# A state-space block with a mixture-of-experts FFN on one core: all eight experts for every token, against only the two that a token is routed to

## Chip, core and metric

The kernel runs on one core of one Trainium2 chip. The metric is the device time of one execution in microseconds (us).

## The reference, cut to what matters

```python
# x: (4, 1024, 512) float32, T = 4096 tokens, D = 512, 8 experts of 256 hidden units, top 2
mod = (_silu(L0_c) @ L0_wmod).reshape(4, 6, 1, -1)       # sa, ca, ga, sb, cb, gb
h = _layernorm(x) * (1 + ca) + sa
x = x + ga * _L0_attn_ref(h, ...)      # conv of 4 taps, projections, softplus, then a scan over
                                       # the 1024 tokens: h = dA * h + dBu, 16 states per channel
h = _layernorm(x) * (1 + cb) + sb
x = x + gb * _L0_ffn_ref(h, ...)

# _L0_ffn_ref
logits = jnp.tanh(xt @ Wg1.T) @ Wg2.T
_, top_idx = jax.lax.top_k(logits, 2)
top_scores = jax.nn.softmax(top_logits, axis=1)
scores = jnp.zeros_like(logits).at[rows, top_idx].set(top_scores)
up = jnp.einsum('td,ehd->teh', xt, Wup) + bup            # every expert for every token
h = jax.nn.silu(up)
down = jnp.einsum('teh,eoh->teo', h, Wdown) + bdown
out = jnp.einsum('te,teo->to', scores, down)             # six of eight scores are zero
```

## The kernel before

The 4096 tokens are cut into 8 chunks of 512 (`NC`), each with two half chunks `cs` of 256 tokens for the FFN (`NF` = 16). The state-space part ("attention" in the code) of a chunk has 64 slots: 16 states times 4 blocks of 128 channels. In a slot ScalarE makes the decay by an exponential into a bank of PSUM (`da`, L1065), GpSimd multiplies `DU` with the broadcast row `BR` into one of four `DB` buffers (`dbu`, L837), VectorE scans both over the 512 tokens (`scan`, L1297), TensorE transposes the result in four pieces (`flip`, L1563), and VectorE multiplies and adds it to `ACC` (`acc`, L1322). The last chunk is split: two scans of 256 in each slot (L1302).

All engines walk one list, `order`, made by `schedule()`: a task stands at a half slot `h`, and 128 half slots (2 W) are one chunk of the scan. Every engine takes its own tasks out of the list in that order and waits on semaphores for the others. So a task that waits holds up whatever stands behind it on its engine; on SyncE this is the queue of all DMAs. Positions are written out by hand in tables: `ATTENTION` for the next chunk's preparation (convolution, projections), `ROUTER` for layer norm, transposes and the gate of a half chunk, `PAIR`/`PAIRS` for its FFN.

The FFN of a half chunk goes expert by expert: for each of 16 blocks `m` of 128 hidden units, `up` (L1612 to L1614) makes the product from weights and tokens split into high and low float32r parts (12 matmuls of 256 columns), ScalarE and VectorE make the SiLU times the token's score (`th` L1167, `t1` L1172, `ys` L1371 with the score row `SR` fetched by a DMA), GpSimd multiplies (`g`, L860), and `dn` (L1642) adds the block into two banks `DN` in float32. For the last blocks `dn` is made of float32r parts instead (`wh`, `wl` L1357, `gh`, `gl` L1363, L1633 to L1635). Then `to` (L1382) applies the gate and `fin` (L865) adds to `ACC`, which a DMA stores. Up weights stay in SBUF; the down weights come again for each half chunk (`WD`, 128 DMAs).

Of the kernel before, what the change touches and what calls it, by code (L numbers as in the profile page):

```python
# [14 lines left out]
LAG = 6
F0 = 24
# [55 lines left out]
    "final": {"fst": (17, 24), "nmf": 26, "fsu": (24, 24), "frs": 26, "fxn": (29, 30), "ftr": (36, 41),
             "fev": (44, 47), "hh": 50, "hl": (49, 61), "r1": 66, "r12": 78, "r2": 82, "r22": 76, "r3": 82,
             "r31": 89, "e1": 91, "r4": 94, "r41": 97, "r42": 97, "sel1": 99, "sel2": 99, "r5": 101, "r52": 101,
             "sw": 103},
    "last": {"fst": (15, 21), "nmf": 26, "fsu": (25, 25), "frs": 31, "fxn": (37, 46), "ftr": (49, 55),
             "fev": (52, 56), "hh": 62, "hl": (58, 64), "r1": 57, "r12": 57, "r2": 58, "r22": 60, "r3": 67,
             "r31": 68, "e1": 67, "r4": 68, "r41": 75, "r42": 75, "sel1": 74, "sel2": 77, "r5": 80, "r52": 79,
             "sw": 80},
    "split": {"fst": (-46, -44), "nmf": -44, "fsu": (-39, -39), "frs": -42, "fxn": (-39, -37), "ftr": (-35, -29),  # L80
             "fev": (-32, -30), "hh": -27, "hl": (-22, -20), "r1": -25, "r12": -24, "r2": -17, "r22": -19, "r3": -19,
             "r31": -19, "e1": -17, "r4": -17, "r41": -16, "r42": -14, "sel1": -12, "sel2": -11, "r5": -9,
             "r52": -12, "sw": -7}}
# [3 lines left out]

PAIR = {"sr": -1, "wd": -4, "up": (0, 2), "th": (4, 4), "ys": (6, 6), "t1": (4, 6), "g": (9, 9), "dn": (12, 14),
        "to": (16, 18), "fin": (18, 22), "out": (17, 25), "gbl": 30, "xa": 25}
FAST = {"sr": -5, "wd": -3, "up": (0, 2), "th": (3, 3), "ys": (4, 4), "t1": (3, 3), "g": (4, 6), "dn": (10, 13),  # L90
        "to": (14, 14), "fin": (19, 27), "out": (35, 35), "gbl": 21, "xa": 21}
TAIL = {"sr": -9, "wd": -11, "up": (-2, -1), "th": (3, 3), "ys": (6, 7), "t1": (4, 5), "g": (7, 7), "dn": (1, 14),
        "to": (16, 19), "fin": (18, 21), "out": (12, 29), "gbl": -4, "xa": 37}
PAIRS = [47, 54, 63, 73, 81, 89, 97, 108, 114, 122, 129, 137, 146, 153, 162, 167]
FAST_PAIRS = [48, 61, 66, 72, 78, 85, 89, 94, 105, 111, 118, 124, 128, 136, 151, 163]
# [1588 lines left out]
```

## Time and profile before

| | |
|---|---|
| time, median of 2 runs | 1391.43 us (1390.89 to 1391.97) |
| span of the profiled execution | 1389.7 us, so the runs shown lie 1.2 to 2.3 us above it |
| busy PE, DVE, POOL, ACT | 94%, 88%, 82%, 71% |
| first scan starts, last scan ends | 43.7 us, 1253.9 us |
| mean granted TensorE clock | 0.977 of 2.4 GHz |

Busy times of PE count matmuls to their modelled ends and overlap each other. The time of a piece on PE is better read from the distance of starts.

### The profile page before, as it was taken

Reading aid. Unit: us, or ns where it says so; the run is one execution under the profiler, and the core shown is the slowest. Engines: PE = TensorE matmul, PEld = TensorE weight load, DVE = VectorE, ACT = ScalarE, POOL = GpSimd, SP = SyncE. Lnnn points to the kernel's source line nnn. Section 1 sums busy time; section 2 is a strip of 40 time slices with the busy share of each in tenths; the row PEclk is TensorE's granted clock in tenths of the full one; section 3 lists DMA queues with packets and bytes.
Section 4 is the critical chain, followed back from the end, with each engine's and each line's share of the span. In section 5 each row is a group of like instructions: output and inputs, shape, how many; then the busy total and the mean of one; then the engine's idle time right before and its main releaser. Section 6 shows DMA issues by size and latency. Waiting matters only on the chain. (4 is left out here: it accounts for less than half of the span.)

```text
span 1389.7 us, 23827 instructions
## 1 busy us (share of the span) xinstructions
PE 1310.4 (94%) x7664; PEld 977.8 (70%) x7664; DVE 1228.5 (88%) x1729; ACT 988.3 (71%) x2110; POOL 1136.4 (82%) x1177
## 2 busy tenths in 40 slices
PE   8888768999999999999999999999999999989998
PEld 4466546767776777777776777767776776768897
DVE  4899999989998999989998999999998999885565
ACT  4875786588857786588858786688758775745654
POOL 1799889799997999799998999799988987762332
PEclk9999867999999999999999999999999999999999
DMA  5542112325342424434342434334253423323342
GB/s 201 177 154 62 61 39 90 115 78 170 94 148 86 161 97 123 132 111 156 90 144 85 164 97 125 125 113 146 87 148 100 129 85 116 108 74 125 112 125 79
DMA packets 99284, 160.94 MB, mean 116 GB/s; under 512 B 9276, under 2 KB 33980, under 8 KB 99160
## 3 DMA queue, kind: packets, MB, share of 16 engines
q1 hardware_dynamic: 99160, 159.42, 36.3%
q8 instruction: 61, 1.00, 0.3%
q14 instruction: 63, 0.52, 0.1%
HBM read 150.60 MB, written 8.79 MB: 115 GB/s over the span
## 5 line engine op out<-in xcount | busy, mean ns | idle before, releaser
L837 POOL TENSOR_TENSOR DB<-DU,BR 128x512 f32<-128x512 f32 x448 | 576.6, 1304 | 43.6 <-DVE H L1297 36.7
L1322 DVE SCALAR_TENSOR_TENSOR ACC<-pb,CTM,ACC 128x512 f32<-128x512 f32 x512 | 373.6, 730 | 42.4 <-PE pb L1563 41.5
L1642 PE MATMUL pb<-WD,G 128*128 128x512 f32 x856 | 406.0, 594 | 0.0
L1065 ACT ACTIVATE pb<-DELP,AN 128x512 f32<-128x512 f32 x448 | 305.8, 685 | 107.5 <-DVE H L1297 105.3
L1563 PE MATMUL pb<-ID,H 128*128 128x128 f32 x2048 | 311.9, 280 | 32.9 <-DVE ACC L1322 25.3
L1563 PEld LDWEIGHTS pb<-ID,H 128*128 128x128 f32 x2048 | 244.0, 144 | 137.0 <-issue 77.5
L1612 PE MATMUL pb<-H2H,WUH 128*128 128x256 f32 x1024 | 326.7, 319 | 12.0 <-DVE TY L1371 11.8
L1297 DVE TENSOR_TENSOR_SCAN H<-pb,DB 128x512 f32<-128x512 f32 x256 | 309.7, 1211 | 13.4 <-ACT pb L1065 12.3
L1614 PE MATMUL pb<-H2H,WUL 128*128 128x256 f32 x1024 | 290.5, 284 | 0.0
L1613 PE MATMUL pb<-H2L,WUH 128*128 128x256 f32 x1024 | 290.2, 283 | 0.0
L860 POOL TENSOR_TENSOR G<-TY 128x256 f32<-128x256 f32 x256 | 188.9, 756 | 99.7 <-ACT TY L1172 44.3
L1297 DVE TENSOR_TENSOR_SCAN H<-pb,ST,DB 128x512 f32<-128x512 f32 x192 | 244.1, 1271 | 7.3 <-ACT pb L1065 7.3
L1642 PEld LDWEIGHTS pb<-WD,G 128*128 128x128 f32 x856 | 149.3, 191 | 108.7 <-issue 107.5
L1612 PEld LDWEIGHTS pb<-H2H,WUH 128*128 128x128 f32 x1024 | 196.3, 192 | 36.2 <-issue 26.4
L1167 ACT ACTIVATE TY<-pb,BUPH 128x256 f32<-128x256 f32 x256 | 108.8, 469 | 149.5 <-PE pb L1614 137.2
L1613 PEld LDWEIGHTS pb<-H2L,WUH 128*128 128x128 f32 x1024 | 196.9, 192 | 13.3 <-issue 12.7
L1614 PEld LDWEIGHTS pb<-H2H,WUL 128*128 128x128 f32 x1024 | 196.2, 192 | 0.0
L1371 DVE SCALAR_TENSOR_TENSOR TY<-pb,BUP,SR 128x256 f32<-128x256 f32 x256 | 110.5, 472 | 35.7 <-ACT TY L1167 32.8
L1172 ACT ACTIVATE TY<-TY 128x256 f32<-128x256 f32 x256 | 102.1, 412 | 0.0
L1302 DVE TENSOR_TENSOR_SCAN H<-pb,ST,DB 128x256 f32<-128x256 f32 x128 | 88.4, 732 | 6.4 <-ACT pb L1070 4.3
L840 POOL TENSOR_TENSOR DB<-DU,BR 128x512 f32<-128x512 f32 x64 | 81.2, 1281 | 4.1 <-DVE H L1302 4.1
L1256 DVE SCALAR_TENSOR_TENSOR U<-DELP,PV,U 128x512 f32<-128x512 f32 x57 | 59.6, 1059 | 0.8
(220 smaller groups left out, 1700.0 us busy)
## 6 DMA issues: line engine op xcount, KB each, us to landing
WD<-in_wdT SPq DMA_DIRECT2D x128, 512.0 KB, 4.7
BR<-bscr SPq DMA_DIRECT2D x112, 256.0 KB, 3.7
SR<-sscr SPq DMA_DIRECT2D x128, 128.0 KB, 4.6
ACC<-in_x SPq DMA_DIRECT2D x16, 512.0 KB, 4.0
out<-ACC SPq DMA_DIRECT2D x32, 256.0 KB, 3.0
DU<-in_x SPq DMA_DIRECT2D x7, 1024.0 KB, 5.6
BR<-bscr SPq DMA_DIRECT2D x32, 128.0 KB, 3.1
DU<-in_xpT SPq DMA_DIRECT2D x7, 320.0 KB, 3.1
```

What stands on the lines that cost most here:

```text
L837: eng.tensor_tensor(DB[:, i % NDB], DU[:, c % 2, r], BR[:, n % 2], ALU.mult).then_inc(S["dbu"], 1)
L860: eng.tensor_tensor(G[:, i % NG], TH[:, m % 2], YS[:, m % 2], ALU.mult).then_inc(S["g"], 1)
L1065: eng.activation(DA[i % NDA][:], DEL[:, c % 2, r], ACT.Exp, scale=AN[:, r, n:n + 1]).then_inc(S["da"], 1)
L1167: eng.activation(TH[:, m % 2], up_of(cs, m), ACT.Tanh, scale=0.5, bias=BUPH[:, m:m + 1]).then_inc(S["th"], 1)
L1297: eng.tensor_tensor_scan(H[:, (c * NS + n) % NH, r], DA[i % NDA][:], DB[:, i % NDB], ST[:, n, r:r + 1] if state_from(c, h) else 0.0, ALU.mult,
L1322: eng.scalar_tensor_tensor(out=acc, in0=banks[bank_of["flip", c, n, r]][:], scalar=1.0 if n < 0 else CTM[:, c % 2, j, st:st + 1], in1=acc, ...
L1371: eng.scalar_tensor_tensor(out=YS[:, m % 2], in0=up_of(cs, m), scalar=BUP[:, m:m + 1], in1=SR[:, m // 2 % 2], op0=ALU.add, op1=ALU.mult).t ...
L1563: t = eng.transpose(b[:, dt * 128:dt * 128 + 128], src[:, dt, r * 128:r * 128 + 128], ID[:])
L1612: eng.matmul(b, WUH[:, kk, sl], H2H[:, cs % 2, kk], start=kk == 0, stop=False)
L1613: eng.matmul(b, WUH[:, kk, sl], H2L[:, cs % 2, kk], start=False, stop=False)
L1614: t = eng.matmul(b, WUL[:, kk, sl], H2H[:, cs % 2, kk], start=False, stop=kk == 3)
L1642: eng.matmul(DN[j][:], G[:, (cs * NM + m) % NG, j * 128:j * 128 + 128], WD[:, (cs * NE + m // 2) % NWD, m % 2], start=False, stop=m == NM ...
```

## The change

The FFN is made only for the chosen pairs of token and expert. The 16 half chunks form 6 groups (4, 4, 4, 2, 1 and 1 half chunks; `GROUPS`). When a group is routed, VectorE and TensorE work out for each of its two choices a row number such that the rows of one expert fill slots of 128 (`s1` to `s8`, `rk`), and GpSimd scatters each block of 128 tokens twice, 2064 bytes a row (the normed token and its score), into a DRAM buffer `xdr` by indirect DMA (`sc`). A group has as many tiles of 128 rows as it can need at worst: 23, 23, 23, 15, 11 and 11, together 106. For each tile: load (`xl`), transpose (`xt`, `xe`), bias and 4 float32 matmuls of 256 columns (`up`, `uq`) against weights that lie in SBUF at an address read from a register (`tile_expert`), tanh and product for two tiles at once (`th`, `gg`), transpose (`gt`, `ge`), bias and 2 float32 matmuls of 512 columns (`dn`, `dq`), scaling by the score (`ye`) and store to `ydr` (`yst`). Then for every block of 128 tokens GpSimd gathers the two results by indirect DMA, the second adding to the first (`yg`), multiplies by the gate (`zm`) and adds to `x` (`fin`); `x` was parked in DRAM for chunks 0 to 5 (`x1s`, `xr`). The high and low splits, the score rows and the DMAs of the down weights are gone.

```diff
+GROUPS = ((0, 1, 2, 3), (4, 5, 6, 7), (8, 9, 10, 11), (12, 13), (14,), (15,))
+SORT = {"e0": 2, "e1": 3, "e2": 5, "e3": 6, "s1": 2, "s2": 4, "rk": 5, "s3": 7, "s4": 8, "s5": 9, "s6": 10, "s7": 11, "s8": 13,
+        "c1": 14, "c2": 14, "c3": 15, "c4": 15, "sc0": 15, "e4": 22, "sc1": 24}
+SORT_AT = (50, 50, 50, 50, -22, 50)
+TILE = {"xl": (0, 2), "xt": (8, 10), "xe": (11, 13), "up": (15, 17), "uq": (16, 18), "th": 21, "gg": 24, "gt": 27, "ge": 30,
+        "dn": (33, 36), "dq": (34, 37), "ye": (37, 40), "yst": (41, 44)}
+PAIRS = ([335, 351, 367, 383, 399, 415, 431, 447, 463, 479, 495, 511],
+         [590, 606, 622, 638, 654, 670, 686, 702, 718, 734, 750, 766],
+         [845, 855, 865, 875, 885, 895, 905, 915, 925, 935, 945, 955],
+         [970, 980, 990, 1000, 1010, 1020, 1030, 1040],
+         [1055, 1065, 1075, 1085, 1095, 1105],
+         [1118, 1128, 1138, 1148, 1158, 1168])
+BACK = {"yg0": 0, "xr": 0, "yg1": 4, "zm": 8, "fin": 9, "out": 11}
+BACKS = ([556, 562, 568, 574, 580, 586, 592, 598],
+         [811, 817, 823, 829, 835, 841, 847, 853],
+         [1000, 1006, 1012, 1018, 1024, 1030, 1036, 1042],
+         [1085, 1091, 1097, 1103],
+         [1150, 1156],
+         [1213, 1219])
...
+    return (256 * len(tokens(g)) + NE * 127) // 128
...
+        if what in ("sc0", "sc1"):
+            at += [(h + t // 2, ("sc", g, int(what[2]), t)) for t in range(len(tokens(g)))]
...
+        def tile_expert(g, i):
+
+            return nc.values_load(EID[0:1, g, i:i + 1], engines=[mybir.EngineType.PE], min_val=0, max_val=(NE - 1) * 1024,
...
+                elif what == "xl":
+                    g, i = k
+                    m = tile_no(g, i)
+                    if i == 0:
+                        eng.wait_ge(S["d_sc"], 16 * scatters(g + 1))
...
+                    eng.indirect_dma_start(out=xdr[g % NXD][0:128 * n_tiles(g), :],
+                                           out_offset=bass.IndirectOffsetOnAxis(ap=POS[:, g, way, t:t + 1], axis=0),
+                                           in_=HT[:, t], in_offset=None).then_inc(S["d_sc"], 16)
...
+                    if way:
+                        eng.wait_ge(S[f"d_g{b % 2}"], 32 * (b // 2) + 16)
...
+                    if way:
+                        eng.indirect_dma_start(out=Z[:, b % 2], out_offset=None, in_=rows, in_offset=at_rows,
+                                               compute_op=ALU.add).then_inc(S[f"d_g{b % 2}"], 16)
...
+                elif what == "zm":
+                    g, t = k
+                    b = back_no(g, t)
+                    eng.wait_ge(S[f"d_g{b % 2}"], 32 * (b // 2 + 1))
...
+                elif what == "e4":
+                    g = k[0]
+                    n = len(tokens(g))
+                    eng.wait_ge(S["d_sc"], 16 * (scatters(g) + n))
...
+                elif what == "up":
+                    g, i = k
+                    m = tile_no(g, i)
...
+                    first = tile_expert(g, i)
+                    if i % 2 == 0:
+                        eng.wait_ge(S["gg"], pair_no(g, i // 2))
+                    eng.wait_ge(S["xe"], m + 1)
+                    b = UPB[:, i % 2 * FT:i % 2 * FT + FT]
+                    eng.matmul(b, OHT[:, g, i:i + 1].to_broadcast([64, 128]), BRW[:, 0:FT], start=True, stop=False)
+                    for kk in range(2):
+                        eng.matmul(b, XTS[:, m % 2, kk], WU[:, bass.ds(first + kk * FT, FT)], start=False, stop=False)
...
+                elif what == "dn":
+                    g, i = k
+                    m, p = tile_no(g, i), pair_no(g, i // 2)
+                    first = tile_expert(g, i)
+                    if m:
+                        eng.wait_ge(S["ye"], m)
+                    eng.wait_ge(S["ge"], p + 1)
+                    b = DN[:]
+                    eng.matmul(b, OHT[:, g, i:i + 1].to_broadcast([64, 128]), BRW[:, FT:FT + D], start=True, stop=False)
+                    eng.matmul(b, GT[:, p % 2, 2 * (i % 2)], WD[:, bass.ds(first, D)], start=False, stop=False)
```

`uq` and `dq` read the register again (4 reads for each tile, 424 in all) and make the rest of the matmuls.

## Rows read from the trace of the kernel before

**Rows 1.** Part 1 of the page: busy time of each engine.

```profile
PE 1310.4 (94%) x7664; PEld 977.8 (70%) x7664; DVE 1228.5 (88%) x1729; ACT 988.3 (71%) x2110; POOL 1136.4 (82%) x1177
```

**Rows 2.** Busy time by stretch: chunks 1, 3 and 7, the tail, chunk 0.

```profile
core 0: us, PE busy (x) PEld busy (x) DVE busy (x) ACT busy (x) POOL busy (x), PEclk, DMA share, GB/s
172.40:317.10 144.70, 123.72 (x683) 91.44 (x684) 137.01 (x178) 108.90 (x216) 128.74 (x130) 0.86 0.28 87
471.50:625.00 153.50, 151.16 (x898) 112.41 (x898) 144.70 (x193) 116.12 (x240) 142.63 (x148) 1.00 0.38 124
1087.00:1253.90 166.90, 158.20 (x899) 114.56 (x898) 152.29 (x271) 103.19 (x267) 130.41 (x140) 0.98 0.35 106
1253.90:1389.70 135.80, 129.88 (x811) 113.70 (x810) 76.58 (x136) 75.84 (x189) 43.14 (x54) 1.00 0.35 112
43.70:172.40 128.70, 104.06 (x641) 79.45 (x640) 120.52 (x133) 92.41 (x166) 117.22 (x102) 0.93 0.37 118
```

**Rows 3.** The same view, the start of chunk 1, before its first FFN matmul.

```profile
172.40:205.00 32.60, 21.80 (x98) 14.36 (x99) 32.60 (x39) 28.69 (x62) 27.11 (x31) 0.65 0.12 34
```

**Rows 4.** Timeline of DVE in chunk 0: start, duration, instruction.

```profile
78.72 1.21 DVE L1297 TENSOR_TENSOR_SCAN H<-pb,DB 128x512 f32<-128x512 f32 x1
79.86 0.73 DVE L1322 SCALAR_TENSOR_TENSOR ACC<-pb,CTM,ACC 128x512 f32<-128x512 f32 x1
80.50 1.21 DVE L1297 TENSOR_TENSOR_SCAN H<-pb,DB 128x512 f32<-128x512 f32 x1
```

**Rows 5.** Group of DVE: busy us, mean ns, idle before.

```profile
L1371 DVE SCALAR_TENSOR_TENSOR TY<-pb,BUP,SR 128x256 f32<-128x256 f32 x256 | 110.5, 472 | 35.7 <-ACT TY L1167 32.8 <-DMA SR<-sscr 2.7
```

**Rows 6.** Groups of POOL.

```profile
L837 POOL TENSOR_TENSOR DB<-DU,BR 128x512 f32<-128x512 f32 x448 | 576.6, 1304 | 43.6 <-DVE H L1297 36.7 <-DVE DU L1279 6.1 <-DMA BR<-bscr 0.6
L860 POOL TENSOR_TENSOR G<-TY 128x256 f32<-128x256 f32 x256 | 188.9, 756 | 99.7 <-ACT TY L1172 44.3 <-DVE TY L1371 42.2 <-PE pb L1642 8.7
L808 POOL TENSOR_TENSOR H2L<-XT,H2H 128x512 fp32r<-128x512 f32 x32 | 40.7, 1290 | 8.3 <-DVE H L1302 5.0 <-ACT H2H L1118 3.3
L562 POOL TENSOR_SCALAR S<-IO,IXF,RS 128x104 f32<-128x104 f32 x28 | 20.6, 746 | 0.0
```

**Rows 7.** Pieces of the chain that ended last: start us, us, what.

```profile
1212.36 0.44 PE pb L1572 x4
...
1215.38 1.72 PE pb L1642 x4
1217.10 1.82 PE pb L1582 x8
```

**Rows 8.** Timeline of PE: float32r matmuls, 256 columns, then 512 columns.

```profile
646.26 0.28 PE L1613 MATMUL pb<-H2L,WUH 128*128 128x256 f32 x1
646.38 0.28 PE L1614 MATMUL pb<-H2H,WUL 128*128 128x256 f32 x1
...
1381.03 0.39 PE L1634 MATMUL pb<-WDL,GHL 128*128 128x512 f32 x1
1381.26 0.40 PE L1635 MATMUL pb<-WDH,GHL 128*128 128x512 f32 x1
```

**Rows 9.** DMA issues: KB each, us to landing; then one issue on SyncE's timeline.

```profile
out<-ACC SPq DMA_DIRECT2D x32, 256.0 KB, 3.0
bscr<-H SPq DMA_DIRECT2D x1, 32.0 KB, 1.6
...
645.58 0.32 SPq L644 DMA_DIRECT2D BR<-bscr  x1
```

**Rows 10.** The last pieces of the chain that ended last.

```profile
1385.62 0.70 DVE XT L1382
1386.35 0.69 DVE ACC L1386
```

**Rows 11.** Who waited for whom: us in total, times, longest.

```profile
ACT TY L1167 <- PE pb L1614: 137.2, 72, 5.6
POOL DB L837 <- DVE H L1297: 36.7, 59, 1.3
```

More of the change, by code:

```diff
@@ L72 @@
[L72 to L95, printed above, removed]
@@ L167, in attention_places, with group_of, tokens, place_of @@
     return at
+def group_of(cs):
+    return next(g for g, of in enumerate(GROUPS) if cs in of)
+def tokens(g):
+    return [(cs, j) for cs in GROUPS[g] for j in range(2)]
+def place_of(cs, j):
+    return tokens(group_of(cs)).index((cs, j))
+def n_tiles(g):
+    return (256 * len(tokens(g)) + NE * 127) // 128
+def n_pairs(g):
+    return (n_tiles(g) + 1) // 2
+def tiles_of(g, q):
+    return range(2 * q, min(2 * q + 2, n_tiles(g)))
+def pair_no(g, q):
+    return sum(n_pairs(x) for x in range(g)) + q
+def tile_no(g, i):
+    return sum(n_tiles(x) for x in range(g)) + i
+def back_no(g, t):
+    return sum(len(tokens(x)) for x in range(g)) + t
+def bounced(cs):
+    return cs // 2 < NC - 2
+def scatters(g):
+    return sum(2 * len(tokens(x)) for x in range(g))
 def router_places(cs):
     at = []
-    kind = "even" if cs % 2 == 0 else "last" if cs // 2 == NC - 2 else "odd"
-    if cs // 2 in SPLIT:
-        kind = "final" if cs % 2 else "split"
+    kind = "odd" if cs % 2 else "split" if cs // 2 in SPLIT else "even"
     for what, places in ROUTER[kind].items():
+        if what == "x1s" and not bounced(cs):
+            continue
         if isinstance(places, tuple):
@@ L180, in router_places, with group_places @@
     return at
+def group_places(g):
+    at = []
+    for what, h in SORT.items():
+        h += SORT_AT[g] + 2 * W * (GROUPS[g][-1] // 2 + 1)
+        if what in ("sc0", "sc1"):
+            at += [(h + t // 2, ("sc", g, int(what[2]), t)) for t in range(len(tokens(g)))]
+        else:
+            at.append((h, (what, g)))
+    at.append((max(PAIRS[g][0] + 16, PAIRS[g - 1][-1] + 42 if g else 0), ("xs", g)))
+    if g in (1, 2, 3):
+        at.append((BACKS[g][0] - 4, ("gbl", g)))
+    for q, b in enumerate(PAIRS[g]):
+        for what, h in TILE.items():
+            if isinstance(h, tuple):
+                at += [(b + h[i % 2], (what, g, i)) for i in tiles_of(g, q)]
+            else:
+                at.append((b + h, (what, g, q)))
+    for t, (cs, _) in enumerate(tokens(g)):
+        for what, h in BACK.items():
+            if what == "xr" and not bounced(cs):
+                continue
+            h += BACKS[g][t]
+            at.append((h, ("yg", g, t, int(what[2])) if what in ("yg0", "yg1") else (what, g, t)))
+    return at
@@ L436, in adaln_kernel @@
                 early = at[EMPTIED[what][0], *k] < at["scan", 1, 0, 0]
-                b = min(range(2, 7) if early else range(2, 5), key=lambda b: last[b])
+                b = min(range(2, 7) if early else WORK_BANKS, key=lambda b: last[b])
                 bank_of[task], freed[task] = b, held[b]
@@ L709, in _ @@
+            for q in range(2):
+                eng.wait_ge(S[f"d_o{q}"], 16 * 2 * NC)
             eng.wait_ge(S["d_bw"], 16 * NC)
-            eng.wait_ge(S["d_sw"], 16 * NF)
         @block.gpsimd
```

886 lines of the change are left out of this document (450 added, 436 removed).

## The prediction

> **What bounds the kernel now.** I read the shares of busy time first [rows 1]: PE, DVE and POOL all stand above 80%, so the page alone names no bound. The view by stretch tells more [rows 2]. I cut it at the first scan of each chunk. The reader is to see three regimes: chunk 0, without FFN, 128.7 us; chunk 1, with half an FFN, 144.7; chunks 2 to 6, of which chunk 3 stands for all, some 154 each; then the split last chunk, 166.9; and after the last scan a tail of 135.8 with nothing but FFN. With the 43.7 us of the head that is the span of 1389.7.
>
> PE's busy time overstates, so I price its work by the distance of starts. A float32 matmul of 512 columns takes 0.86 us (two in 1.72), one of 256 columns 0.455 (four in 1.82), a block of four transposes 0.44 [rows 7]; a float32r matmul takes 0.12 at 256 columns and 0.23 at 512 [rows 8]. Counting the list, chunk 3 has 32 `up` x 12 x 0.12 = 46, 64 `dn` x 0.86 = 55, 68 `flip` x 0.44 = 30, and some 11 for the rest: 142 of 154 us. DVE is busy 144.7 and POOL 142.6 in the same stretch. So three engines share the bound, and ACT waits for PE (137 us in total) while POOL waits for the scan (37) [rows 11]. Taking the FFN from PE alone would give only what DVE and POOL allow.
>
> What DVE allows can be read off. Where it never idles, one slot takes 80.50 - 78.72 = 1.78 us (1.14 scan, 0.64 acc) [rows 4]. At the start of chunk 1, before its FFN, DVE is busy for all of 32.6 us although the granted clock is 0.65, a mixture of 1.2 and 2.4 GHz [rows 3]: an idle PE and its slow clock cost the scan nothing there. 64 slots, 5 accs of the skip term and 7 of the convolution give 64 x 1.78 + 5 x 0.64 + 7 x 0.9 + 5 = 128 us for a chunk without FFN, which chunk 0 confirms (128.7 with 8 us of starting stalls and less preparation).
>
> **The change, part by part.** All sums are against the span of 1389.7.
>
> *PE work.* A tile costs `up`+`uq` 4 x 0.455 + 0.12 = 1.94, `dn`+`dq` 2 x 0.86 + 0.23 = 1.95, transposes 0.44 + 0.22: 4.55 us. 106 tiles are 482 us, against 16 x (256 / 16 x 12 x 0.12 + 32 x 0.86) = 809 before. The saving is 40%, not 75%: the worst-case number of tiles is 106 where 64 full ones would do, and the tiles run in float32.
>
> *Where the tiles lie.* From the list: chunk 1 has none, chunks 2 to 7 have 5, 16, 8, 16, 9 and 23 `up`, and 29 `up` and 33 `dn` come after the last scan. In chunks 2 to 6 PE has at most 16 x 4.55 + 30 + 12 = 115 us, so it is no bound. In chunk 7 it has 23 x 4.55 + 30 + 12 = 147, and the tail is PE's again.
>
> *DVE.* `ys` goes (110.5 / 256 = 0.43 each, 14 of the 144.7 us of a full chunk [rows 5]), and `to` (4 x 0.7 [rows 10]). It gains `gg`, 0.65 for two tiles, and about 20 small ones of 0.15 for each sort, 3 us. So chunk 1 gets its floor, 128 + 2 = 130 (-15). Chunks 3 and 5, with 8 `gg`, get 128 + 5 + 1 for the gate + 5 idle, the half of what it idles today: 139 (-15 each).
>
> *POOL.* `g` goes (32 x 0.74 = 24 a chunk), the low parts (4 x 1.29 = 5) and the selection (8 of about 0.75 and small ones, 8) [rows 6]: 142.6 falls to 106. It gains `zm`, 1.3 each, and 128 indirect DMAs. No row shows one. Call its time on POOL X. The lower bound is SyncE's issue of a plain DMA, 0.32 us; the upper is a whole landing of 256 KB, 3.0 [rows 9]. I take 1.1, between POOL's passes over 256 and 512 columns (0.76 and 1.30 [rows 6]), since an entry must be made for each of 128 rows on both sides. The Trainium skill, DMA: Bandwidth & Descriptors, section SWDGE vs HWDGE vs iDMA, says that GpSimd's processor computes the entries in a program loop, with slower setup than the queues that hardware serves; no run here shows that yet. By that page's fit of 2.0 us + bytes / 436e3 a block of 256 KB would land after 2.6 us, an estimate; the landing of 3.0 in rows 9 is what I use.
>
> These DMAs come in bursts, in time order with the `dbu` that the scan needs, and `dbu` is only two slots ahead. *Scatter of 8 blocks:* eight stand within 4 half slots, then `e4` on DVE, 7 half slots after the first, waits for all eight to land, with the scans queued behind it. POOL needs 8 X + 3.5 x 1.27 for `dbu` + 3.0 to land; DVE would be there after 7. Stall 8 X + 0.4 less about 1 for the start = 8.2. The other eight: 8 X + 4.4 against 7 and two slots of lead (3.6): 2.6. Together some 11. *Gather of 8 blocks:* in the 53 half slots of `BACKS` POOL has 27 `dbu` (34 us), 8 `zm` and 8 `fin` (21), 3 of small ones and 16 X = 18, together 76, where DVE needs 27 x 1.78 + 6 = 54 and the lead is worth 5: stall 17 us. The scatters of the next group stand in the same stretch and add to it.
> Chunk 2: 128 + 1 + 3 + 4 idle + 11 = 147 (-7). Chunks 4 and 6: 128 + 3 + 3 + 4 + 11 + 17 = 166 (+12 each). So POOL eats up in every second chunk what PE and DVE give in the others.
>
> *Chunk 7.* PE 147, and some idle as today (166.9 with a like sum of 141 + 8): DVE loses `wl`, `gl` and `ys`, so PE's sum decides more nearly: 156 (-11).
>
> *Tail.* PE after the last scan: 33 x 1.95 + 29 x 1.94 + 27 x 0.44 + 17 x 0.44 + 7 flips, router and `rk` 6 = 146. Today's tail has 41 x 1.44 for `up` and 88 `dn` of mostly 0.69, some 130 in all, and ends 4.7 us after the last matmul [rows 7, 8, 10]: it measures 135.8, so PE runs there with almost no stall. The new end is longer: `ye` 0.6, store 3.0, two gathers one behind the other 2 x (X + 2.2), two rounds of `zm` and `fin` 5, the other block's gather 3, the last store 3: 21 us. With 7 for the waits of group 5's routing, which PE passes in its fixed order: 174 (+38).
>
> *Hidden at nothing:* loading and zeroing (69 stores of 264 KB in chunks 0 to 2) lie on a DMA share of 0.35 [rows 2]; without that cover they would cost about 1 us each. In `up` and `dn` the reads of the register stand ahead of the waits, so they run while PE works off what is queued. Their price is in no row: the lower bound is 0, the upper the shortest trip to memory and back, 1.6 us [rows 9], for some 4 x 54 = 216 reads in chunk 7 and the tail. I take 0. The Trainium skill, Runtime: NRT & Kernel Launch, section Instruction fetch mechanics, gives about 200 ns for loading one register, which the sequencer waits for; if all of these were exposed, 216 x 0.2 = 43 us would come on top, an estimate, and no row shows it.
> SyncE: `xl` waits for the scatters and `out` for `fin`, with the `BR` rows of the scan queued behind; these are fetched 4 slots early (7 us), which covers it while POOL is late by no more.
>
> **Sum.** -15 - 7 - 15 + 12 - 15 + 12 - 11 + 38 = -1: span 1389, time 1390. That is no change.
>
> **Rivals.**
> 1. *Indirect DMAs are cheap on POOL* (X about 0.32 to 0.6). At 0.32: scatter 3, gather 4, so chunk 2 139, chunks 4 and 6 144 each, chunk 7 153, tail 170: -15 - 15 - 15 - 10 - 15 - 10 - 14 + 34 = -60, 1330; at 0.6 about 1351. For it: SyncE's 0.32 for a DMA of the same size. Against it: the row numbers must be read and worked on.
> 2. *Register reads and addresses from registers stall PE* (slower). If each of the 4 reads for a tile holds PE for 0.5 us, chunk 7 and the tail get 216 x 0.5 = 108 longer, chunks 3 and 5 become PE's with 115 + 32 against 139, 8 each: 1390 + 108 + 16 = 1514; at 0.2, 1433. It decides from about 0.12 us each. For it: PE has no slack in the tail today. Against it: the reads precede the waits.
> 3. *X is large, or POOL's waits chain* (slower). At X = 1.8 scatter costs 23 and gather 28: +4, +34, +34, with chunk 7 -5 and the tail +42, 1455. It decides from X = 1.4. The wait of the second gather for the first, with `dbu` behind it, works in the same sense.
> 4. *The clock falls* in chunks 1 and 2, where PE does little. Rows 3 show it at 0.65 with DVE never idle, so I give it no price.
> That fewer tiles are computed than before is certain from the list, so "it doesn't do what it says" is no case.
>
> **How the numbers follow.** Forecast 0.38, rival 1 0.30, rival 2 0.17, rival 3 0.15. The range takes in rival 1's low end and rival 3 and the lower part of rival 2: 1325 to 1465. The forecast's own range is 1365 to 1415. Two per cent is 28 us: faster by more than that 0.33, within it 0.34, slower 0.33.
>
> **What the profile after would show.** Right: chunks 3 and 5 near 139 and DVE almost without idle; chunks 4 and 6 longer than 154, with DVE's idle put down to POOL's `dbu`; an idle of DVE at `e4` released by a DMA; PE back to back in the tail, and some 20 us from its last matmul to the end. It would be wrong if the indirect DMA takes under 0.6 or over 1.5 us on POOL, if PE has gaps at each `up`/`dn` in the tail, or if the tail is under 160.

## The result, and the profile after

The changed kernel takes 1595.24 us (1594.51 to 1595.98, two runs), against 1391.43 before (1390.89 to 1391.97): a ratio of 1.146, 95% interval 1.144 to 1.149. The forecast was 1390 us, its range 1325 to 1465. The profiled execution's span is 1592.8 us.

Part 1 of the page, busy shares, to be held against [rows 1]:

```profile
PE 1211.0 (76%) x5756; PEld 829.7 (52%) x5756; DVE 1128.7 (71%) x1489; ACT 931.1 (58%) x1772; POOL 1027.0 (64%) x936
```

All engines are busy for less time than before, in a longer span: the loss is waiting. The view by stretch says where, one row for each chunk and the last for the tail, against [rows 2]; columns as there:

```profile
43.30:173.60 130.30, 104.29 (x644) 81.77 (x643) 119.37 (x133) 84.86 (x158) 97.52 (x86) 0.90 0.65 194
173.60:303.30 129.70, 86.29 (x391) 61.95 (x390) 127.27 (x154) 94.22 (x168) 102.46 (x92) 0.68 0.45 147
303.30:461.40 158.10, 102.94 (x491) 75.95 (x492) 133.99 (x174) 100.64 (x194) 119.80 (x111) 0.73 0.32 97
461.40:632.50 171.10, 148.03 (x716) 101.02 (x715) 136.00 (x163) 118.04 (x215) 101.48 (x92) 0.94 0.29 97
632.50:829.60 197.10, 118.37 (x553) 84.53 (x551) 140.75 (x175) 105.94 (x204) 157.52 (x140) 0.74 0.42 121
829.60:990.70 161.10, 141.20 (x714) 96.05 (x713) 137.49 (x162) 117.75 (x215) 102.18 (x93) 0.98 0.32 106
990.70:1191.80 201.10, 122.39 (x585) 86.96 (x585) 145.11 (x177) 107.61 (x208) 158.87 (x141) 0.79 0.44 126
1191.80:1376.80 185.00, 174.65 (x862) 118.95 (x860) 144.70 (x263) 116.37 (x263) 104.24 (x98) 0.98 0.39 116
1376.80:1592.80 216.00, 174.26 (x657) 104.14 (x656) 19.90 (x50) 60.49 (x112) 75.72 (x65) 0.92 0.48 137
```

Measured against forecast: chunk 0 130 (129, as before), chunk 1 130 (130), chunk 2 158 (147), chunk 3 171 (139), chunk 4 197 (166), chunk 5 161 (139), chunk 6 201 (166), chunk 7 185 (156), tail 216 (174). Against before the differences are +2, -15, +4, +18, +43, +7, +47, +18 and +80: with the head, which is as long as before, the 203 us by which the span grew. Two patterns are to be seen. In chunks 4 and 6 POOL is the busiest engine (157.52 and 158.87 us) while PE has 118 and 122. In chunks 3, 5 and 7 PE is the busiest: 148, 141 and 175. The granted clock is lower than before as well: chunk 3 had 1.00 and has 0.94, the tail 1.00 and 0.92.

The waits (who waited for whom, total us, times, longest) name both:

```profile
DVE ACC L1376 <- PE pb L1668: 104.3, 79, 4.7
DVE H L1351 <- POOL DB L914: 78.7, 29, 9.4
...
POOL Z L902 <- DMA Z<-ydr,POS: 36.3, 15, 3.5
...
ACT YO L1221 <- DMA ydr<-YO: 35.2, 6, 9.6
...
DVE HT L1422 <- DMA xdr<-HT,POS: 24.6, 5, 7.9
```

The scan's wait for `DB` is new in kind; before, POOL waited for the scan [rows 11]. POOL's groups price the indirect DMA, which no row of before showed (scatter; gather that adds; gather that doesn't; busy us, mean ns, idle before):

```profile
L872 POOL DMA_INDIRECT xdr<-HT,POS x64 | 63.4, 990 | 38.6 <-issue 28.5 <-DVE POS L1462 3.7 <-DVE H L1356 2.9
L891 POOL DMA_INDIRECT Z<-ydr,POS x32 | 51.6, 1612 | 18.9 <-DMA Z<-ydr,POS 12.9 <-issue 4.0 <-DVE HT L1422 0.2
L894 POOL DMA_INDIRECT Z<-ydr,POS x32 | 33.6, 1050 | 85.5 <-issue 49.1 <-DMA ydr<-YO 30.2 <-ACT DU L1045 6.1
```

The DMA issues, against [rows 9] (median us to landing at the end):

```profile
xdr<-HT,POS POOLq DMA_INDIRECT x64, 3.7
Z<-ydr,POS POOLq DMA_INDIRECT x64, 5.0
```

POOL's timeline in chunk 4 shows how they meet the scan (start, us, instruction, idle before):

```profile
748.13 1.87 POOL L914 TENSOR_TENSOR DB<-DU,BR 128x512 f32<-128x512 f32 x1
750.17 1.00 POOL L894 DMA_INDIRECT Z<-ydr,POS  x1 [0.16 <-issue]
...
755.36 0.97 POOL L872 DMA_INDIRECT xdr<-HT,POS  x1 [0.30 <-issue]
756.36 1.27 POOL L914 TENSOR_TENSOR DB<-DU,BR 128x512 f32<-128x512 f32 x1
```

and DVE's timeline the scan that was kept waiting:

```profile
757.83 1.22 DVE L1351 TENSOR_TENSOR_SCAN H<-pb,DB 128x512 f32<-128x512 f32 x1 [5.92 <-POOL DB L914]
```

Five indirect DMAs, a gather of one group and four scatters of the next, stand between two `dbu`: 6.4 us of POOL, and DVE idles for 5.92.

### The profile page after: what moved, and what is told of

The parts are those of the page before. It is cut to its first block and busy times, and to the rows that moved or that the text cites. A ratio compares the mean times of both kernels' runs of the same rounds, so it can differ in the third digit from the quotient of the medians.

```text
span 1592.8 us, 20071 instructions
## 1 busy us (share of the span) xinstructions
PE 1211.0 (76%) x5756; PEld 829.7 (52%) x5756; DVE 1128.7 (71%) x1489; ACT 931.1 (58%) x1772; POOL 1027.0 (64%) x936
## 5 line engine op out<-in xcount | busy, mean ns | idle before, releaser
L1668 PE MATMUL pb<-ID,H 128*128 128x128 f32 x2048 | 360.2, 313 | 184.6 <-DVE ACC L1376 146.9
L1221 ACT ACTIVATE YO<-pb,SCO 128x512 f32<-128x512 f32 x106 | 72.3, 682 | 164.4 <-PE pb L1771 129.0
L1490 DVE SCALAR_TENSOR_TENSOR TH<-TH,pb 128x512 f32<-128x512 f32 (+1 forms) x56 | 36.2, 646 | 133.1 <-ACT TH L1203 133.1
L1741 PE MATMUL pb<-WU,XTS 128*128 x424 | 127.2, 425 | 0.0
L1766 PE MATMUL pb<-WD,GT 128*128 x212 | 123.5, 665 | 0.0
L1748 PE MATMUL pb<-WU,XTS 128*128 x424 | 114.9, 395 | 0.0
L1771 PE MATMUL pb<-WD,GT 128*128 x212 | 110.2, 602 | 0.0
L1748 PEld LDWEIGHTS pb<-WU,XTS 128*128 128x128 f32 x424 | 83.7, 201 | 35.0 <-issue 26.0
L1724 PE MATMUL pb<-ID,XS 128*128 128x128 f32 x424 | 66.5, 284 | 31.2 <-DMA XS<-xdr 14.8
L894 POOL DMA_INDIRECT Z<-ydr,POS x32 | 33.6, 1050 | 85.5 <-issue 49.1
L872 POOL DMA_INDIRECT xdr<-HT,POS x64 | 63.4, 990 | 38.6 <-issue 28.5
L1741 PEld LDWEIGHTS pb<-WU,XTS 128*128 128x128 f32 x424 | 76.2, 200 | 21.1 <-issue 2.0
L1724 PEld LDWEIGHTS pb<-ID,XS 128*128 128x128 f32 x424 | 51.7, 146 | 46.5 <-issue 25.8
L1765 PE MATMUL pb<-BRW,OHT 64*128 64x512 f32 x106 | 53.2, 501 | 28.2 <-ACT YO L1221 23.0
```

The costliest lines, as they stand in the source:

```text
L1668: t = eng.transpose(b[:, dt * 128:dt * 128 + 128], src[:, dt, r * 128:r * 128 + 128], ID[:])
L1724: t = eng.transpose(b[:, dt * 128:dt * 128 + 128], XS[:, m % NXS, dt * 128:dt * 128 + 128], ID[:])
L1741: eng.matmul(b, XTS[:, m % 2, kk], WU[:, bass.ds(first + kk * FT, FT)], start=False, stop=False)
L1748: t = eng.matmul(b, XTS[:, m % 2, kk], WU[:, bass.ds(first + kk * FT, FT)], start=False, stop=kk == 3)
L1766: eng.matmul(b, GT[:, p % 2, 2 * (i % 2)], WD[:, bass.ds(first, D)], start=False, stop=False)
L1771: eng.matmul(DN[:], GT[:, p % 2, 2 * (i % 2) + 1], WD[:, bass.ds(first + D, D)], start=False, stop=True).then_inc(S["dn"], 1)
```

## The experiments

Each kernel is the changed one with one edit, unless said otherwise. Times compare with 1595.24; all but the last are single runs, and before, on the same chips, gave 1390.03 to 1392.68, so that a few us of the whole time say nothing. In the diffs "..." shortens a line. I quote the time from the first scan of a chunk to that of the next.

**1. Register reads.** The offset of the expert's weights is a constant, not read from memory.

```diff
-            return nc.values_load(EID[0:1, g, i:i + 1], ...)
+            return i % NE * 1024
```

> Leaves out the choice of the expert: each tile takes its weights at a constant address (tile number modulo 8) where the changed kernel reads a register four times a tile; all else stays, so the output is another. Theory A (register reads and register addresses hold PE up in chunk 7 and in the tail, where a pair of tiles takes 10.45 us against 9.1 by the prices of the kernel before): the pair falls to about 9.2 us, tail and chunk 7 together lose some 27 pairs x 1.2 = 32 us, the time some 1560. Rival (the reads run ahead of PE's queue and cost nothing): within 4 us of 1595.

1595.35 us, chunk by chunk within 2 us of the changed kernel. Rival 2 is dead: the reads cost nothing. The Trainium skill, Runtime: NRT & Kernel Launch, section Instruction fetch mechanics, gives about 200 ns for such a load; all exposed, that would be 43 us, an estimate. The runs show none of it: the loads are hidden here, most likely since PE's sequencer runs ahead (argued, not shown).

**2. The bias matmuls.** Both are left out.

```diff
-                    eng.matmul(b, OHT[:, g, i:i + 1].to_broadcast([64, 128]), BRW[:, 0:FT], start=True, stop=False)
-                    eng.matmul(b, OHT[:, g, i:i + 1].to_broadcast([64, 128]), BRW[:, FT:FT + D], start=True, stop=False)
```

> Leaves out the two bias matmuls of each tile (212 float32r matmuls with a stationary operand of 64 rows). In the trace the bias of 512 columns holds PE for 0.43 us and that of 256 columns for 0.30, where I had counted 0.23 and 0.12, and the float32 matmul behind it takes 0.2 more than its twin. Theory B (these switches are what the tile costs above my price): a pair of tiles loses 2 x (0.43 + 0.30 + 0.3) = 2 us, 10.45 to about 8.4, tail and chunk 7 some 50 us less, 1545. Rival (PE is held by waits for other engines in the tail, not by its own work): under 20 us.

1531.41 us: 64 less for two instructions priced at 0.35 us a tile together, which would be 37 for all 106. Chunk 3 falls from 171 to 152, chunk 5 from 161 to 148. That is below theory B's 1545; some of chunk 3's fall is the clock's (0.94 before the edit, 0.97 with it; see edit 6). PE's work stands in the way in these chunks, and the matmuls cost more than their own time.

**3. Bias on 128 rows.** They use 64 of the array's rows, all others 128. This kernel widens them, with zeros in the added rows.

```diff
-        BRW = sb("BRW", [64, FT + D], f32r)
+        BRW = sb("BRW", [128, FT + D], f32r)
-        OHT = sb("OHT", [64, len(GROUPS), 23], f32r)
+        OHT = sb("OHT", [128, len(GROUPS), 23], f32r)
-    ...to_broadcast([64, 128])
+    ...to_broadcast([128, 128])
```

> The same work; the one-hot and the bias rows have 128 rows instead of 64 (rows 64 to 127 are zero), so that the bias matmuls use the whole array like their neighbours. Without them a pair of tiles took 8.08 us instead of 10.45 in the tail, 1.18 a tile where two float32r matmuls of 256 and 512 columns should take 0.35. Theory B1 (the change of the array's rows between 64 and 128 keeps PE from loading the next weights ahead): the pair falls to about 9, the time by some 40 us to 1555. Rival B2 (the change between float32r and float32, or the broadcast stationary operand, does it): 10.4 and 1595 as before.

1546.35 us, 49 less, with the same number of instructions and columns. PE's timeline in the tail of the changed kernel:

```profile
1542.29 0.38 PE L1739 MATMUL pb<-BRW,OHT 64*128 64x256 f32 x1
1542.60 1.13 PE L1741 MATMUL pb<-WU,XTS 128*128 x4
1543.66 0.49 PE L1765 MATMUL pb<-BRW,OHT 64*128 64x512 f32 x1
1544.08 1.13 PE L1766 MATMUL pb<-WD,GT 128*128 x2
1545.04 1.03 PE L1748 MATMUL pb<-WU,XTS 128*128 x4
```

and the like place with 128 rows:

```profile
1500.79 0.36 PE L1739 MATMUL pb<-BRW,OHT 128*128 128x256 f32 x1
1500.99 1.02 PE L1741 MATMUL pb<-WU,XTS 128*128 x4
1501.86 1.03 PE L1748 MATMUL pb<-WU,XTS 128*128 x4
...
1503.08 0.48 PE L1765 MATMUL pb<-BRW,OHT 128*128 128x512 f32 x1
1503.39 1.02 PE L1766 MATMUL pb<-WD,GT 128*128 x2
1504.25 1.02 PE L1771 MATMUL pb<-WD,GT 128*128 x2
```

From start to start the `dn` bias takes 0.42 us with 64 rows (1543.66 to 1544.08) and 0.31 with 128, the two matmuls behind it 0.96 and 0.86; the `up` bias 0.31 and 0.20, the four behind it 1.06 and 0.87. That is 0.51 us a tile for these places alone. The matmuls ahead of a bias are stretched too, as the distance of two pairs of tiles in the tail shows, with nothing else between. A pair took 10.45 us (the rows are given further down); with 128 rows it takes 9.02, as theory B1 had said:

```profile
1480.25 0.47 PE L1765 MATMUL pb<-BRW,OHT 128*128 128x512 f32 x1
...
1489.27 0.48 PE L1765 MATMUL pb<-BRW,OHT 128*128 128x512 f32 x1
```

So the switch costs 0.7 us a tile, 76 us for 106 tiles, and PE's busy time falls by as much, from 1211.0 to 1135.0. Of these 76 us 49 show in the time, and a few of them are the clock's, in chunk 3. They don't show in the tail, which is only 2.4 us shorter although PE is busy there for 155.88 us in place of 174.26. PE's wait for `ye` (YO) takes up the rest, in the tail of the changed kernel and of this one:

```profile
PE pb L1765 <- ACT YO L1221: 11.5, 6, 6.4
PE pb L1765 <- ACT YO L1221: 28.0, 8, 11.8
```

ScalarE in its turn waits there for the stores to `ydr`, 35.2 us before this edit and 48.2 with it.

**4. Where the gate runs.** `zm` and `fin` go, unchanged, from POOL's block of code to DVE's.

```diff
 @block.gpsimd
-                elif what == "zm": ...
-                elif what == "fin": ...
 @block.vector
+                elif what == "zm": ...
+                elif what == "fin": ...
```

> The same work, but the gate product and the final add of each block (64 instructions of 1.28 us) go from POOL to DVE, where each takes about 0.65 to 0.7. Theory C (POOL is the bound in chunks 4 and 6): POOL sheds 16 x 1.28 = 20 us in each, DVE gains 11 in a stretch where it idles 55: chunks 4 and 6 about 183 each, the end of the tail 2 us shorter, time about 1563. Rival (DVE's own order matters more: it now waits for the gather in front of the scans): no gain, 1590 or more.

1571.80 us, 23 less; chunks 4 and 6 fall by 6 and 7, half of the 14 expected, the tail by 8.

**5. Plain moves.** Scatters and gathers become plain DMAs of the same blocks to and from fixed rows, issued by SyncE; the sorting and the addition are left out, and the second scatters of group 3 stand up to one half slot earlier, so that SyncE doesn't wait for a store that is behind it in its own queue.

```diff
-  gpsimd: eng.indirect_dma_start(out=xdr[...], out_offset=...POS..., in_=HT[:, t])
+  sync:   eng.dma_start(xdr[g % NXD][r0:r0 + 128, :], HT[:, t])
-  gpsimd: eng.indirect_dma_start(out=Z[:, b % 2], in_=ydr, in_offset=...POS..., compute_op=ALU.add)
+  sync:   eng.dma_start(Z[:, b % 2], ydr[g][r0:r0 + 128, :])
```

> Leaves out the sorting of rows and the adding gather: the same 64 stores and 64 loads of 128 rows are plain DMAs on SyncE's queue at constant rows, with the same waits (the second stores of group 3 stand up to one half slot earlier, so that SyncE doesn't wait for its own later stores), and the second load of a block overwrites the first. The bytes are the same, POOL has no DMA. Theory C (in chunks 4 and 6 POOL is the bound, with 32 indirect DMAs of 1.0 to 1.6 us ahead of the products that the scan needs): chunks 4 and 6 fall from 197 and 198 to about 160, chunk 2 from 158 to about 148, the time some 1510. Rival (the loss is the waits of these blocks for one another and for their landing, whoever issues): chunks 4 and 6 stay above 185.

1489.47 us, 106 less, and 21 less than expected. Chunk 2 falls by 17, chunks 4 and 6 by 33 each (to 164 and 168), the tail by 27; chunk 3 stays at 171. It is the largest single cause.

**6. The clock.** The transposes of the scan's results are issued twice in the chunks of low clock (1, 2, 4, 6), so that PE rests less.

```diff
-                    for dt in range(4):
+                    for _ in range(2 if c in (1, 2, 4, 6) and n >= 0 else 1):
+                        for dt in range(4):
```

> The same work; in chunks 1, 2, 4 and 6, where the granted clock is 0.68, 0.73, 0.74 and 0.78, each block of four transposes of the scan's state is made twice, so that PE is busier and the clock should stand near 1. Theory D (the low clock lengthens PE's pieces and so the waits of acc for PE): chunks 2 and 6 lose the 8 and 12 us that DVE waits for PE there, time about 1575. Rival (in these chunks DVE waits for POOL, and the clock costs nothing, as I had said): within 6 us of 1595 or slower, with the clock near 0.95.

1607.62 us at a mean granted clock of 0.913, against 0.859: theory D's 20 us don't come, and the time rises by 12. In chunk 1, where DVE hardly waits for PE, the clock goes from 0.68 to 0.89 and the time from 129.7 to 130.2, so the low clock cost nothing there. Elsewhere this run can't price the clock, since `acc` now waits for the second set of transposes as well: its wait for PE grows from 8.3 to 10.8 us in chunk 2 and from 12.6 to 17.8 in chunk 6.

Other traces can. `late_out`, the next kernel, is the same in chunks 3 and 5. Each pair of rows holds the same scans, first in the changed kernel, then in `late_out`: slots 8 to 24 of chunk 3, and the end of chunk 5 from slot 56 on, ahead of which both take 144.00 us.

```profile
479.70:529.60 49.90, 44.34 (x217) 30.13 (x215) 37.17 (x48) 39.04 (x72) 28.02 (x30) 0.90 0.25 81
476.60:522.40 45.80, 39.86 (x216) 26.82 (x214) 37.06 (x48) 38.99 (x72) 28.13 (x30) 1.00 0.26 89
973.60:990.70 17.10, 15.24 (x75) 10.01 (x74) 15.65 (x17) 11.80 (x20) 16.42 (x15) 0.98 0.42 136
966.30:986.60 20.30, 18.44 (x75) 11.54 (x74) 15.70 (x18) 11.83 (x20) 16.50 (x15) 0.82 0.36 114
```

DVE, ACT and POOL have the same busy times to 0.2 us, PE has the same work and needs 4.5 and 3.2 us more for it at the lower mean clock, and the stretch is longer by 4.1 and 3.2. (The mean clock mixes two levels, 1.2 and 2.4 GHz.) So where the scan waits for PE, the low clock does cost time. It costs 7 us of chunk 3: 171.1 at a mean of 0.94, 164.3 at 0.98. What makes the clock fall in one run and not in the other is open, as the work ahead of the end of chunk 5 is the same in both.

**7. Later stores.** The stores to `out` stand 10 half slots later in the list for the groups after the third, so that SyncE's queue isn't held for `fin`.

```diff
-            h += BACKS[g][t]
+            h += BACKS[g][t] + (10 if what == "out" and g > 2 else 0)
```

> The same work; the last stores of groups 3 to 5 stand 10 half slots later in SyncE's queue. In the tail SyncE waits for the final add of POOL in front of each of these stores (69 us in all), and the tile stores behind it land late; ScalarE waits for them (35 us) and PE for ScalarE. Theory E (this chain through SyncE's queue is what PE's gaps of 0.9 to 2.0 us in the tail after 1450 us are): tail 5 to 10 us shorter, 1587. Rival (PE's own sum sets the tail): within 2 us of 1595, or slower, since the stores of the last group come later.

1584.61 us, 11 less: 7 in the tail, and 7 in chunk 3, where the edit changes nothing and the clock stands higher, as said. Kernels that are alike in chunk 3 show 171 at 0.94, 168 (`gate_on_dve`, `pool_time`) at 0.97 and 164 at 0.98. Only the tail's part is the edit's.

**8. The ledger.** `mended` joins edits 3, 4 and 7 (with the stores and `xr` of the other groups 4 half slots later); `mended_plain` adds edit 5.

> The changed kernel with the bias rows and one-hots on 128 partitions (alone -49 us), zm and fin on VectorE (alone -23 us) and the output stores placed later in the list (alone -11 us), all at once. If the three act on separate stretches, the time is 1595 - 49 - 23 - 11 = 1512 us. If they shorten the same waits, it saves less than the sum: the largest alone gives 1546 us, and anything from 1530 to 1546 says that they overlap.

1521.39 us: 74 less, where the parts alone add up to 83, between the two readings. The 23 and 11 of edits 4 and 7 hold 4 and 7 us of chunk 3 that are the clock's. In the tail the three give more together than apart, 23 against 2 + 8 + 7: most likely the cheaper bias pays there once the stores no longer hold ScalarE up.

> The same three edits, and the scatter and the gather as plain DMAs of the same sizes issued by SyncE (alone -106 us; it leaves out the sorting, so rows go to and come from fixed places). If the four causes add up, the time is 1595 - 106 - 49 - 23 - 11 = 1406 us, within 15 us of the kernel before, and then the whole loss is accounted for. If GpSimd's queue and VectorE's moves relieve the same wait, gate on VectorE gives nothing more here or costs, and the time is 1430 to 1450 us.

1430.62 us, 165 less than the changed kernel, where the parts add up to 189: not the 1406 of causes that add up, but the edge of the second reading, and still 38 more than before (1392.68). Against before, its chunks 0 to 7 differ by +2, -15, -15, +1, +9, -4, +16 and +9, the tail by +35 (forecast +38 in the kernel with all causes in it).

**9. Fewer tiles.** The last two half chunks are routed and sorted as one group, on top of `mended`: 99 tiles in place of 106.

```diff
-GROUPS = ((0, 1, 2, 3), (4, 5, 6, 7), (8, 9, 10, 11), (12, 13), (14,), (15,))
+GROUPS = ((0, 1, 2, 3), (4, 5, 6, 7), (8, 9, 10, 11), (12, 13), (14, 15))
```

> The kernel of the run mended, with the last two half chunks routed and sorted together, as one group of 15 slots in place of two of 11: 99 tiles in place of 106. Theory: the tail is bound by tiles of TensorE and by the waits around each group, so that seven tiles less at 4.3 us or so save 30 us and one group end less saves another 10 to 20 us: 40 to 50 us less than the run mended. Rival: the first tile can begin only when the last chunk is routed, and the work of the half chunk 14 no longer lies beside chunk 7: the tail gets longer by 11 tiles of 4.3 us less what is saved, and the time is about that of mended, or up to 20 us above.

1523.60 us against 1521.39: the rival was right. Chunk 7 falls from 177 to 175, the tail rises from 193 to 200. PE starts no bias of a tile in the tail from 1371.9 to 1403.2 us, for 31 us in which the joined group is routed and sorted. The tail's granted clock is 0.81 too, against 0.92, so some of the 7 us may be the clock's. Seven tiles less are worth no more than that.

**10. Why do the indirect DMAs cost 106 us?** First by kind, each alone made plain (the diffs of edit 5, one at a time).

> The changed kernel with the 64 scatters alone as plain DMAs of the same size from SyncE, at fixed places (sorting left out; the gathers stay indirect, on GpSimd). With scatters and gathers both plain the time was 1489 us, 106 less. The scatters take 64 x 1.29 = 83 us of GpSimd in chunks 2, 4, 6 and 7. If GpSimd's time beside the scan is the cause, chunks 4 and 6 fall by most of the 33 and 30 us of the run with both, and the time is 1530 to 1550 us. If it is the chain of gathers, this gives under 20 us.

> The 64 gathers alone as plain DMAs from SyncE (no addition; the scatters stay indirect, on GpSimd). If the two parts add up, the times of this run and of the one with plain scatters lie together 106 us below twice 1595 us. The gathers are 64 of about 1.3 + 0.3 us, 105 us of GpSimd, most of them in chunks 4 to 7 and the tail: I expect 1535 to 1560 us, most of it in chunk 4, in chunk 6 and at the end of the tail.

1539.41 and 1533.26 us: 56 and 62 less, 118 against 106 for both together. Chunk 4 falls by 20 and 20 against 33 for both: the two meet in the same stretch. In chunk 6 they don't overlap, with 12 and 18 against 33.

Then by mechanism. Both are plain, and POOL gets two small instructions at each of the 128 places, without and with the waits.

```diff
 @block.gpsimd
+                elif what in ("sc", "yg"):      # pool_time_waits: the waits of the indirect DMA stand here
+                    for z in range(2):
+                        eng.tensor_tensor(SPC[:, 2 * z:2 * z + 2], ONES[:, 0:2], ONES[:, 0:2], ALU.pow)
```

> Scatters and gathers plain from SyncE as in the run of 1489 us, and at each of the 128 places in GpSimd's order where the changed kernel has an indirect DMA, two small instructions of 0.7 us that wait for no other engine (about 1.4 us; the indirect ones take 1.46 us with the stretch ahead of them, on the mean). If it is the mere time on GpSimd, chunks 4 and 6 rise again from 164 and 168 us to 195 or so, and the time is 1560 us or more. If it is the indirect transfer itself or the waits in front of it, the time stays within 20 us of 1489 us.

> As the run before it, and the small instructions also wait for what the indirect DMAs waited for (the normalized rows, the positions, the stored tiles, the landing of the first gather of a pair). If time and waits together are the whole of it, the time is 1580 to 1600 us, as in the changed kernel. What is left between it and 1595 us is the indirect transfer's own.

1547.93 and 1564.89 us against 1489.47 with neither. The first lies between its two expectations, nearer to mere time: that is worth 58 of the 106 us, and chunks 2, 4 and 6 hold it (154, 191 and 194, where `plain_moves2` has 141, 164 and 168). The waits in front add 17, of which 4 and 3 lie in chunks 3 and 5, where no indirect DMA stands, so that some 10 are left for them. The second time is 15 us short of what "the whole of it" needed: 30 us are left, 22 of them in the tail, for what only an indirect transfer brings.

**11. Was the bound read rightly?** Here the base is the kernel before. `before_less_pe` leaves out the matmul with the low part of h, `before_less_low` its making on POOL as well.

```diff
-                        eng.matmul(b, WUH[:, kk, sl], H2L[:, cs % 2, kk], start=False, stop=False)
# before_less_low also:
-                    eng.tensor_tensor(HLV[cs % 2][:, d], H2F[:, d], HHV[cs % 2][:, d].bitcast(f32), ALU.subtract)
```

> The kernel before, without one of the three matmuls of each tile of the product up (the line with the low part of h), so that the output is that of another precision. It relieves TensorE by 2048 of about 20000 columns of a steady chunk's FFN and takes nothing from another engine, with no new work on GpSimd. If TensorE binds the steady chunks of the kernel before as the prediction took it, a chunk of 154 us falls by its share of TensorE's time, some 5 us, and the whole by 30 to 45 us, to 1345 to 1360 us. If the chunks are bound by VectorE and the chain around it, the time stays within 10 us of 1391 us, and fewer columns had nothing to give there.

> The kernel before, without the low part of h in the product up: the matmul with it (on TensorE) and its making (32 passes of 128x512 on GpSimd, 1.29 us each) are both left out, so that the product is of lower precision in h. Leaving out the matmul alone gave 1342 us, a steady chunk 149 us. If GpSimd shares the bound of the chunks, as the prediction took it, its 5 us a chunk give another 1 to 3 us a chunk, 1320 to 1335 us. If only VectorE and TensorE bind, the time stays at 1340 us.

1342.18 us, and 1333.43 (1332.15 to 1333.64, beside 1392.18 for before, 1389.18 to 1393.02; ratio 0.958, interval 0.956 to 0.960). A steady chunk falls from 154 to 149, then to 148.4. Chunk 3 of `before_less_low`:

```profile
461.20:609.60 148.40, 138.38 (x769) 96.75 (x768) 144.48 (x193) 115.64 (x239) 137.63 (x144) 1.00 0.41 128
```

DVE has 144.48 of 148.40. Taking a third of `up` from PE (4 x 256 columns of 32 blocks, not the 2048 columns of the expectation; 15 us at 0.12 each) gave 5 us a chunk, and 4 x 1.29 = 5 us less on POOL gave 0.6 more. The time of 1333 lies in the range for a POOL that shares the bound, but the 1 to 3 us a chunk behind that range don't come: 4 of the 9 us lie in chunk 7 and the tail. So in the kernel before PE binds a little above DVE's floor, and POOL adds next to nothing in a steady chunk. `before_less_low` is faster than both kernels, at lower precision in `up`.

## Why the prediction was wrong

*Chunk 1 (130, measured 129.7): right, and for the reason given.* DVE is busy for 127.27 of it, at a clock of 0.68.

*The scatter and gather stalls (11 and 17 us): right in mechanism, somewhat too small.* X was taken as 1.1 us. Measured are 0.99 for a scatter, 1.05 for a gather and 1.61 for one that adds, with 0.30 or 0.16 of issue ahead of each: (63.4 + 51.6 + 33.6 + 64 x 0.30 + 64 x 0.16) = 178 us for 128, 1.4 each, just where rival 3 "decides". In the prediction's own formulas 1.4 makes the stalls 16 and 21, and chunk 4 175 us, not 197. Without any indirect DMA chunks 2, 4 and 6 lose 17, 33 and 33 us, where the stalls were forecast as 11, 28 and 28: this term is short by 16 us in all. The other 26 and 30 us by which chunks 4 and 6 of `plain_moves2` (164 and 168) exceed 166 - 28 = 138 belong to the 4 us that the sum set down as idle. DVE waits there 12.0 us for POOL, 6.9 for ScalarE, 5.8 for stores to land and 3.2 for PE in chunk 4, and 14.8 for PE, 9.1 for POOL and 5.6 for stores in chunk 6.

The sum priced the scatters of the next group and the gathers apart and only said that they "add to it"; POOL's timeline and the pair `plain_scatter` and `plain_gather` show them meeting in chunk 4. A gather lands after 5.0 us in the median, where the sum had X + 2.2 = 3.3, and two stand one behind the other at the end of the tail. Pieces of the end of the chain (start, us, what), against [rows 10]:

```profile
1571.26 3.38 DMA Z<-ydr,POS
...
1575.09 4.70 DMA Z<-ydr,POS
...
1582.60 5.02 DMA Z<-ydr,POS
```

From the last matmul's end (1566.57 + 1.02 = 1567.6) to the end of the span are 25 us, where 21 were forecast.

*"In chunks 2 to 6 PE has at most 16 x 4.55 + 30 + 12 = 115 us, so it is no bound": the step that failed.* PE is busy for 148 us in chunk 3 and 141 in chunk 5, and in chunk 3 DVE waits for PE's transposes above all:

```profile
DVE ACC L1376 <- PE pb L1668: 30.1, 15, 3.5
```

Two things are wrong in the step. The first is the size of a tile. In the tail a pair takes 10.45 us, 5.2 a tile, where 4.55 was forecast:

```profile
1529.50 0.49 PE L1765 MATMUL pb<-BRW,OHT 64*128 64x512 f32 x1
...
1539.95 0.50 PE L1765 MATMUL pb<-BRW,OHT 64*128 64x512 f32 x1
```

With 128 rows it is 4.5: the forecast missed the switch of rows, 0.7 us a tile, and nothing else of weight. (The bias matmuls at 0.20 and 0.31 cost 0.16 more than priced, the matmuls of 256 columns a little less.) But 16 x 5.2 + 42 is 125 us, still less than the 136 that DVE is busy, so the size alone wouldn't make PE a bound.

The second fault weighs more: PE's sum was set against DVE's, and the difference called slack. PE takes tiles and transposes in a fixed order, and the scan's chain can't wait for the tiles ahead of a transpose. The trace shows one such wait, in slots 8 to 24 of chunk 3; the scan, what PE does (some lines left out), and the `acc`:

```profile
509.68 1.28 DVE L1351 TENSOR_TENSOR_SCAN H<-pb,ST,DB 128x512 f32<-128x512 f32 x1
511.91 1.02 PE L1771 MATMUL pb<-WD,GT 128*128 x2
512.77 1.03 PE L1748 MATMUL pb<-WU,XTS 128*128 x4
513.63 0.60 PE L1668 MATMUL pb<-ID,H 128*128 128x128 f32 x4
514.34 0.75 DVE L1376 SCALAR_TENSOR_TENSOR ACC<-pb,CTM,ACC 128x512 f32<-128x512 f32 x1 [3.38 <-PE pb L1668]
```

The scan ends at 510.96, its transposes start at 513.63, and PE has worked without a gap since. Laid over PE's instructions, 14 of the 15 waits are of this kind, 27 of the 30.1 us; in the other PE stands for 3.9 us until ScalarE has copied a tile's XTS. The low clock makes such blocks longer, by 7 us of this chunk (experiment 6), where rival 4 gave it no price. `mended`, whose chunk 3 has 133.19 us of PE in 157.0, still has DVE wait 18.1 us for PE there. `plain_moves2`, which leaves chunk 3 at 171.0, shows that the indirect DMAs have no part in it. That the loss of chunk 3 would go if the tiles were spread between the transposes is not shown: no run tried another order.

*Chunk 7 (156, measured 185).* The same step: 147 for PE against 174.65 busy; in `mended` 158.24 busy, and the chunk takes 177.

*Tail (174, measured 216).* The 42 us that were missed have several causes, and the edits alone give 2 to 27 us here. The largest, 27, is the scatters and gathers. The tiles' price is not one by itself (2.4 us for the bias on 128 rows), because of a term that the prediction put at nothing: SyncE's queue, where the stores to `out` wait for POOL's last addition and hold up the tiles' stores, for which ScalarE waits 35.2 us in the tail, six times. Freeing the queue alone gives 7, and the three edits of `mended` 23. All four give 45 (170.6 in `mended_plain`). A gap of 6.4 us ahead of group 5's first tiles came as forecast (7).

*Reads of the register (0): right.*

*Rivals.* Rival 3 was the nearest, with 0.15: X came out at the 1.4 from which it decides, and its chain of gathers came true, but its 1455 held only POOL's share. Against the kernel before the loss is 204 us; taken out one at a time, the scatters and gathers give 106 of it back, PE's switch of rows 49, the gate on POOL up to 23 and SyncE's queue up to 11, and all four 165. The forecast itself held 67 us of stalls in chunks 2, 4 and 6, so the 106 are not all a miss; no rival joined POOL's share with PE's. Open are what makes the clock fall, what divides the last 30 us of the indirect transfers, and the 38 that `mended_plain` keeps, most of it in the tail.

## What to carry to other kernels

A saving of work on one engine is worth only what the next bound allows, and the work that arranges it must be priced where it runs: here a third of the FFN's matmul time (106 x 5.2 = 551 us in place of 809) was paid for with 178 us on the engine that feeds the scan two slots ahead. Before calling an engine free in a stretch, add its work as its new instructions will run, from rows of the same shapes, and ask in what blocks it comes between what others wait for. A granted clock that costs nothing where an engine never waits for PE costs time where it does, so its price is read stretch by stretch. A fault in a sum of many small terms shows best in a run that changes one shape and nothing else.
